# Cross attention on one core: the key projection by seven products instead of eight, in two rounds

## The reference

```python
Q = (input_Q @ W_Q).reshape(b, -1, N_HEADS, D_K).transpose(0, 2, 1, 3)
K = (input_K @ W_K).reshape(b, -1, N_HEADS, D_K).transpose(0, 2, 1, 3)
V = (input_V @ W_V).reshape(b, -1, N_HEADS, D_V).transpose(0, 2, 1, 3)
scores = jnp.einsum('bhqd,bhkd->bhqk', Q, K) / np.sqrt(D_K)
attn = jax.nn.softmax(scores, axis=-1)
context = jnp.einsum('bhqk,bhkd->bhqd', attn, V)
context = context.transpose(0, 2, 1, 3).reshape(b, -1, N_HEADS * D_V)
out = context @ W_O + input_Q
mu, var = jnp.mean(out, axis=-1, keepdims=True), jnp.var(out, axis=-1, keepdims=True)
return (out - mu) / jnp.sqrt(var + 1e-05)
```

## Time and profile before

| | us |
|---|---|
| median of 3 runs | 1601.09 |
| profiled execution, its own time | 1601.11 |
| its span (first to last instruction) | 1599.3 |
| TensorE busy | 1590.5 (99%) |
| VectorE busy | 1314.6 (82%) |
| ScalarE busy | 835.4 (52%) |
| GpSimd busy | 64.2 (4%) |

### The profile page before, as it was taken

How to read it: one execution, slowest core, us unless ns; L and a number is a source line. 1 busy time by engine, 2 the same in 40 slices (tenths; PEclk the granted TensorE clock), 3 DMA queues, 4 the chain that set the end, 5 groups by cost and what they waited for, 6 DMA issues and landing times.

```text
span 1599.3 us, 39500 instructions
## 1 busy us (share of the span) xinstructions
PE 1590.5 (99%) x17484; PEld 1073.0 (67%) x17484; DVE 1314.6 (82%) x1229; ACT 835.4 (52%) x828; POOL 64.2 (4%) x41
## 2 busy tenths in 40 slices
PE   9999999999999999999999999999999999999998
PEld 4576677766777667766677666776677766777435
DVE  7788788887888788887798878988789887888877
ACT  4445554555545555456544565445654455544653
POOL 0001000010000001000010000000000000000100
PEclk9999999999999999999999999999999999999999
DMA  4000000000000000000000000000000000000000
GB/s 162 3 2 9 1 2 9 2 10 1 10 2 1 10 1 10 2 1 9 1 10 2 2 9 2 10 2 2 9 1 10 2 9 2 1 10 2 9 2 15
DMA packets 13006, 14.26 MB, mean 9 GB/s; under 512 B 4784, under 2 KB 8624, under 8 KB 12832
## 3 DMA queue, kind: packets, MB, share of 16 engines
q1 hardware_dynamic: 12544, 11.36, 2.3%
q10 hardware_dynamic: 288, 0.33, 0.1%
HBM read 10.60 MB, written 0.59 MB: 7 GB/s over the span
## 4 chain that ended last, share of the span: by engine, by line
PE 98%; DVE 1%; ACT 0%; issue 0%; DVEq 0%; ACTq 0%
PE o_ps L484 44%; PE s_ps L467 42%; PE w_ps L549 6%; PE w_ps L532 5%; PE s_ps L616 0%; DVE inv_sum L943 0%; DVE y L976 0%; DVE stats L963 0%; PE w_ps L564 0%; DVE y L959 0%; PE w_ps L607 0%; DVE inv_sum L809 0%; DVE sums L835 0%; DVE limits L985 0%; DVE k_all L809 0%
## 5 line engine op out<-in xcount | busy, mean ns | idle before, releaser
L728 ACT ACTIVATE probs<-s_ps 128x1024 f32<-128x1024 f32 x801 | 822.5, 1027 | 737.1 <-PE s_ps L467 737.1
L835 DVE TENSOR_TENSOR sums<-sums,probs 128x1024 f32<-128x1024 f32 x785 | 968.0, 1233 | 213.7 <-ACT probs L728 205.5
L484 PE MATMUL o_ps<-probs,v_all 64*64 64x512 f32 x6408 | 942.9, 589 | 0.0
L467 PE MATMUL s_ps<-q_sb,k_all 64*64 64x512 f32 x6408 | 942.8, 589 | 0.0
L467 PEld LDWEIGHTS s_ps<-q_sb,k_all 64*64 64x64 f32 x6408 | 447.8, 133 | 238.9 <-issue 39.0
L484 PEld LDWEIGHTS o_ps<-probs,v_all 64*64 64x64 f32 x6408 | 424.8, 133 | 204.9 <-issue 33.6
L532 PEld LDWEIGHTS w_ps<-wv_sb,ctx_all 64*64 64x64 f32 x3176 | 122.4, 132 | 30.6 <-issue 1.7
L809 DVE TENSOR_REDUCE k_all<-w_ps 128x512 f32<-128x1024 f32 (+2 forms) x104 | 122.8, 1181 | 16.0 <-PE w_ps L549 14.9
L809 DVE TENSOR_REDUCE v_all<-w_ps 128x512 f32<-128x1024 f32 (+2 forms) x103 | 121.8, 1182 | 15.8 <-PE w_ps L532 15.7
L532 PE MATMUL w_ps<-wv_sb,ctx_all 64*64 64x128 f32 x3176 | 120.0, 269 | 0.1
L549 PE MATMUL w_ps<-ctx_all,wk_sb 64*64 64x512 f32 (+2 forms) x832 | 119.3, 573 | 0.0
(11 more groups left out here) (85 smaller groups left out, 119.5 us busy)
## 6 DMA issues: line engine op xcount, KB each, us to landing
inv_sum<-inv_dram SPq DMA_DIRECT2D x30, 128.0 KB, 2.9
ctx_all<-in_ctxT SPq DMA_DIRECT2D x11, 256.0 KB, 5.1
quad_rows<-quad_sums SPq DMA_DIRECT2D x60, 4.0 KB, 1.8
x_sb<-in_x SPq DMA_DIRECT2D x1, 512.0 KB, 10.1
wo_sb<-in_wo SPq DMA_DIRECT2D x1, 512.0 KB, 11.3
left_rows<-p_left SPq DMA_DIRECT2D x30, 8.0 KB
inv_left<-inv_dram SPq DMA_DIRECT2D x30, 8.0 KB
wq_sb<-in_wq SPq DMA_DIRECT2D x1, 448.0 KB, 6.4
```

The source lines that it names most:

```text
L467: last = nc.tensor.matmul(s_ps[part(half), u % 2, head * QH:(head + 1) * QH], k_all[part(head), c * P + half * DH:c * P + (half + 1) * DH] ...
L484: last = nc.tensor.matmul(o_ps[part(head), rows, :], v_all[part(rows), c, part(head)], probs[part(rows), u % RING, head * QH:(head + 1) * QH],
L728: nc.scalar.activation(probs[:, u % RING, :], s_ps[:, u % 2, :], ACT.Exp, scale=SCALE).then_inc(probs_ready, 1)
L835: nc.vector.tensor_tensor(out=sums[0:rows, t % 2, :], in0=sums[0:rows, t % 2, :], in1=probs[0:rows, u % RING, :], op=ALU.add).then_inc(sum ...
```

## The change

For the pairs 1 to 7 the 12 full key blocks are computed with Strassen's scheme: the product of the weights (2x2 parts of 64x64: input half by head) and the context (2x2 parts: input half by a set of keys) takes 7 products of parts instead of 8, with sums of parts before and differences after. Pair 0 and the tail block stay as they are.

- A block's 14 matmuls of 128 columns come in two rounds: `seven_first` (kind "r", 8 matmuls: 2 on each quarter) and, two steps later, `seven_second` (kind "k", 6 matmuls: one half of the rows has 2 on each of its quarters, the other half 1). Which half has more changes from block to block (`one = b % 2`). The value block moves from c = 2, 6, ... to c = 3, 7, .... First rounds and value blocks stand behind the step's `product`, second rounds ahead of it (`behind`); the tail key block at c = 40 also stands ahead.
- Between the rounds ScalarE copies parts to the other half of the partitions (`cross`, three activations) and GpSimd takes two differences of 128x128 (`sum_crossed`). VectorE evicts with three instructions instead of one (`take_seven`), 256 columns each; the first of them waits for GpSimd's second difference.
- The sums of context parts (`form_keys`, four GpSimd instructions a block) are made once, in pass 0, written to DRAM (`forms_dram`) and loaded again for each pair, 384 KB a block, into two buffers (`c_forms`). The sums of weights (`form_weights`, eight GpSimd instructions a pair) are made at c = 20 of the odd pass before. The new issues stand in SyncE's queue among the old ones.
- VectorE's sums stand one step ahead instead of two (`SUMS_AHEAD = 1`). GpSimd's normalization moves to c = 13 of its order. The chunks within a block change places, and `product` reads the values in the same order (`key_chunk`).

```diff
+    NEXT_STEPS = (0, 36, 38, 40, 41, 42, 44, 45)
+    SUMS_AHEAD = 1
@@ work_at
+            if by_seven(pair, at // 4 + 2) and at % 4 in (0, 2):
+                return ("rk"[at % 4 // 2], pair, at // 4 + 2)
             if at >= 0 and at % 4 == 0 and at // 4 + 2 < BLOCKS:
                 return ("k", pair, at // 4 + 2)
-            if at >= 2 and at % 4 == 2 and at // 4 + 2 < BLOCKS:
+            if at >= 2 and at % 4 == (2 if t == 0 else 3) and at // 4 + 2 < BLOCKS:
                 return ("v", pair, at // 4 + 2)
@@ gpsimd
+            def sum_crossed(pair, b):
+                n = seven_index(pair, b)
+                pool.wait_ge(crossed_ready, 3 * (n + 1))
+                m4, m3, m1 = (1, 2, 3) if b % 2 == 0 else (2, 3, 1)
+                nc.gpsimd.tensor_tensor(out=crossed[:, m4, :], in0=crossed[:, m4, :], in1=crossed[:, 0, :],
+                                        op=ALU.subtract).then_inc(crossed_summed, 1)
+                pool.wait_ge(crossed_summed, 2 * n + 1)
+                nc.gpsimd.tensor_tensor(out=crossed[:, 0, :], in0=crossed[:, m3, :], in1=crossed[:, m1, :],
+                                        op=ALU.subtract).then_inc(crossed_summed, 1)
@@ tensor
+            def seven_first(found):
+                pe.wait_ge(work_ready, READY[found] - 1)
+                pe.wait_ge(w_forms_ready, pair)
+                pe.wait_ge(c_forms_loaded[n % 2], 16 * (n // 2 + 1))
+                for i in range(2):
+                    g = part(1 - i)
+                    nc.tensor.matmul(main[g, 0, 1, :], w_form(one, 0, 1 - i), form(one, pair, b, i, 0), start=True, stop=True)
+                    nc.tensor.matmul(extra[g, 0, :], w_form(two, 5, i), form(two, pair, b, i, 2), start=True, stop=True)
+                for i in range(2):
+                    h = part(i)
+                    at = pair * P + i * DH
+                    nc.tensor.matmul(main[h, 1, 1, :], wk_sb[part(one), at:at + DH], form(one, pair, b, i, 1),
+                                     start=True, stop=True)
+                    last = nc.tensor.matmul(m1[h, :], w_form(two, 3, i), form(two, pair, b, i, 0), start=True, stop=True)
+            def seven_second(found):
+                pe.wait_ge(crossed_ready, 3 * (n + 1))
+                for i in range(2):
+                    nc.tensor.matmul(extra[part(i), 1, :], w_form(two, 4, i), form(two, pair, b, i, 1), start=True, stop=True)
+                for i in range(2):
+                    at = b * BK + 2 * i * P
+                    nc.tensor.matmul(main[part(i), 1, 0, :], w_form(one, 1, i), form(one, pair, b, i, 2), start=True, stop=True)
+                    last = nc.tensor.matmul(main[part(1 - i), 0, 0, :], w_form(one, 2, 1 - i), ctx_all[part(one), at:at + P],
+                                            start=True, stop=True)
+            def behind(found, u):
+                return found[0] in "rv" and by_seven(found[1], 0) and u % FULL_CHUNKS > 0
@@ scalar
+            def cross(pair, b):
+                act.wait_ge(work_done, COUNT["r", pair, b])
+                if n > 0:
+                    act.wait_ge(work_ready, READY["k", pair - (b == 0), (b - 1) % FULL_BLOCKS])
+                for half in range(2):
+                    nc.scalar.activation(crossed[part(1 - half), 1:4, :], apart[part(half), :, :],
+                                         ACT.Copy).then_inc(crossed_ready, 1)
+                nc.scalar.activation(crossed[:, 0, :], seven_slots(b)[2], ACT.Copy).then_inc(crossed_ready, 1)
@@ vector
+            def take_seven(found):
+                dve.wait_ge(work_done, COUNT[found])
+                dve.wait_ge(crossed_summed, 2 * (n + 1))
+                nc.vector.tensor_tensor(out=target[:, :, 0, :], in0=both, in1=main[:, :, 0, :],
+                                        op=ALU.subtract).then_inc(seven_step, 1)
+                nc.vector.tensor_reduce(out=target[:, :, 1, :], in_=main.rearrange("p j s k -> p j k s"), axis=AX.X,
+                                        op=ALU.add)
+                dve.wait_ge(seven_step, n + 1)
+                nc.vector.tensor_tensor(out=target[:, :, 0, :], in0=target[:, :, 0, :], in1=extra,
+                                        op=ALU.subtract).then_inc(work_ready, 1)
```

More of the change, by code:

```diff
@@ L265, in spread_wide, with turned_ctx, form, w_form @@
             return v_wide[part(head), :].rearrange("p (n m) -> p n m", n=PAIRS)[:, :, head * LEFT:(head + 1) * LEFT]
+        def turned_ctx(b):
+            return attn[:, PAIRS - 1, b % 2 * QH:(b % 2 + 1) * QH]
+        def form(half, pair, b, i, n):
+            at = (3 * i + n) * P
+            return c_forms[part(half), seven_index(pair, b) % 2, at:at + P]
+        def w_form(half, n, i):
+            return w_forms[part(half), n, part(i)]
+        def seven_slots(b):
+            other = w_ps[:, 1 - b % 2, :].rearrange("p (n k) -> p n k", k=P)
+            pair_at, m1_at = (2, 1) if b % 2 == 0 else (0, 3)
+            return (w_ps[:, b % 2, :].rearrange("p (j s n) -> p j s n", j=2, s=2),
+                    other[:, pair_at:pair_at + 2, :], other[:, m1_at, :])
         def banks_of(found):
@@ new lines, in store_forms, with load_forms @@
+            def store_forms(b):
+                sp.wait_ge(c_forms_ready, b + 1)
+                sp.dma_start(forms_dram[b, :, :], c_forms[:, b % 2, :]).then_inc(c_forms_stored[b % 2], 16)
+            def load_forms(pair, b):
+                n = seven_index(pair, b)
+                if n < 2:
+                    for slot in range(2):
+                        sp.wait_ge(c_forms_stored[slot], 16 * (FULL_BLOCKS // 2))
+                else:
+                    sp.wait_ge(work_done, COUNT["k", pair - (b < 2), (b - 2) % FULL_BLOCKS])
+                sp.dma_start(c_forms[:, n % 2, :], forms_dram[b, :, :]).then_inc(c_forms_loaded[n % 2], 16)
@@ new lines, in load_turned_w @@
+            def load_turned_w(pair):
+                if pair > 1:
+                    sp.wait_ge(work_done, COUNT["k", pair - 1, FULL_BLOCKS - 1])
+                for half in range(2):
+                    sp.dma_start(w_forms[part(half), 0, :], w_k[part(1 - half), pair * P:(pair + 1) * P]
+                                 ).then_inc(turned_w_loaded, 16)
+            for b in range(2):
+                load_turned(b)
+            for b in range(FULL_BLOCKS):
+                if b == LEFT_BEHIND:
+                    load_left(0)
+                store_forms(b)
+                if b + 2 < FULL_BLOCKS:
+                    load_turned(b + 2)
@@ L365, in _ @@
             sp.wait_ge(left_zeroed, 2)
             for t in range(PASSES - 1):
+                pair, h = (t + 1) // 2, (t + 1) % 2
+                if h == 0:
+                    for b in range(2, 5):
+                        load_forms(pair, b)
                 sp.wait_ge(quad_sums_ready, t + 1)
@@ L384, in _ @@
                     load_left(t + 1)
+                if h == 1 and pair + 1 < PAIRS:
+                    load_turned_w(pair + 1)
+                    for b in range(2):
+                        load_forms(pair + 1, b)
+                if h == 0:
+                    for b in range(6, FULL_BLOCKS):
+                        load_forms(pair, b)
             def general():
@@ L429, in _, with add_halves @@
             nc.gpsimd.memset(inv_left[:, :], 1.0).then_inc(left_zeroed, 1)
-            for t in range(PASSES - 1):
-                pair, h = t // 2, t % 2
+            def add_halves(t):
                 pool.wait_ge(o_a_ready, t + 1)
@@ new lines, in _ @@
+            pool.wait_ge(identity_ready, 2)
+            pool.wait_ge(left_zeroed, 2)
+            for b in range(FULL_BLOCKS):
+                form_keys(b)
+            pool.wait_ge(c_forms_ready, FULL_BLOCKS)
+            for t in range(1, PASSES):
+                for c in range(FULL_CHUNKS):
+                    if c == 0:
+                        add_halves(t - 1)
+                    found = work_at(t, c)
+                    if found is not None and found[0] == "r":
+                        sum_crossed(found[1], found[2])
+                    if c == NORM_STEP:
+                        norm(t - 1)
+                    if c == W_FORMS_STEP and t % 2 == 1 and t // 2 + 1 < PAIRS:
+                        form_weights(t // 2 + 1)
@@ L628, in _ @@
                     left_work(found)
-                elif found is not None:
-                    work(found)
+                elif found is not None and not behind(found, u):
+                    project(found)
                 product(u)
+                if found is not None and behind(found, u):
+                    project(found)
             work(("d", PASSES - 1, 0))
@@ L908, in _ @@
                 take(found)
-            for u in range(AHEAD):
+            for u in range(SUMS_AHEAD):
                 add_sums(u)
```

166 lines of the change are left out of this document (136 added, 30 removed).

## The result

| | before | after |
|---|---|---|
| median, same chip | 1601.05 us (12 runs) | 1604.46 us (12 runs) |
| ratio, 95% interval | | 1.0021 [1.0013, 1.0029] |
| profiled execution, its span | 1601.11, 1599.3 | 1603.05, 1601.3 |

A forecast was written before the change was run, and what follows sets the result against it. The prediction took TensorE, busy 99% of the span, as the bound. Its terms -3.3 + 5.6 + 4.8 + 1.8 + 1.3 = +10.2 us took 1601.1 to about 1611 us, range 1598 to 1625.

The forecast's parts named there:

- columns removed: TensorE's 84 key blocks: the half of the rows done first runs ahead (the lead), saving 0.04 a block, -3.3 us.
- tail key block: At c = 40 TensorE waits 0.80 us for the value block's eviction in each of 7 even passes, +5.6 us.
- VectorE in even passes: VectorE's extra work delays evictions in steps 2 to 11, two waits making 0.69 us a pass, +4.8 us (0 to 12).
- c = 42 of odd passes: The left-over row's sum delays a value block's eviction, so the next first round stands 0.25 us, +1.8 us (0 to 4).
- `form_keys` in pass 0: 48 GpSimd instructions among VectorE's sums, which they exclude, cost +1.3 us (0 to 12).
- what limits the lead: TensorE's wait for the value block's eviction: possible after 2.54 us, due after 2.60, so 0.05 of 0.11 comes through.
- The third rival: A faster hand-over from eviction to matmul carries the lead whole (-7.8), VectorE's waits mostly vanish: 1596 us, chance 0.12.
- four steps at 8.49 or less: Sign in the middle of an even pass that the lead is whole; the forecast itself had 8.55 us.
- The second wait: In steps 4 to 11 of even passes, from fold and inversion: assumed as large as the first, 0.34 us.
- Rival 1: TensorE's strict order or costlier short matmuls: nothing saved, 1.4 in place of -3.3, 1616 us, chance 0.15.
- Rival 2: VectorE and GpSimd lock each other, 0.25 us lost per block, 21 us more: 1632 us, chance 0.14.
- Rival 4: Tail stall as computed, lead whole, no other stalls: 1600 us; or a 3.3 gain without later stalls: 1604; chance 0.14.

The follow-up runs named there:

- e1: The changed kernel with the tail key block of pairs 1 to 7 moved from c = 40 to c = 41: 1598.33 us, ratio 0.9983 to the kernel before.
- e8: The changed kernel with GpSimd's two differences between the rounds narrowed from 128 to 8 columns (keys wrong): 1601.97 us, ratio 1.0007 to the kernel before.
- e11: e1 with only the left-over row moved, to c = 30 of even and c = 44 of odd passes: 1597.55 us, ratio 0.9978 to the kernel before.
- e9: The kernel before with VectorE's sums one step ahead instead of two, nothing else changed: 1600.44 us, ratio 0.9998.
- e12: e11 with the transpose also moved from c = 2 to c = 3: 1601.23 us, ratio 1.0003 to the kernel before.
- e2: The changed kernel with the same half of the rows heavier in every block, no exchange (keys wrong): 1609.72 us, ratio 1.0057 to the kernel before.
- e3: The changed kernel with the second round's two matmuls of the lighter half issued twice: 1613.29 us, ratio 1.0081 to the kernel before.
- e4: The changed kernel with the four GpSimd sums per block in pass 0 replaced by writes of zeros (keys wrong): 1603.64 us, ratio 1.0018 to the kernel before.
- e5: The changed kernel with VectorE's sums two steps ahead again: 1614.39 us, ratio 1.0088 to the kernel before.
- e7: e1 with transpose, fold, inversion, GpSimd's normalization and left-over row moved to later steps: 1621.3 us, ratio 1.013 to the kernel before.

## Why the prediction was wrong

Per pair, in us: the lead gives 12 x 0.09 = 1.08. Of the waits, e1 shows 0.84 for the tail, e8 and the steps 0.32 for c = 4, e11 against e1 0.16 for c = 42. 195.43 - 195.03 + 1.08 = 1.48 are there in all, so 0.16 is left for c = 7, 11 and 16 (the longer steps there show 0.42; the steps behind them are up to 0.16 shorter than their like, which fits a half that catches up where only the other one stood, but no run tested it). Times 7, beside the forecast:

| term | forecast | measured |
|---|---|---|
| columns removed | -3.3 | -7.6 |
| tail key block | +5.6 | +5.9 |
| VectorE in even passes | +4.8 | +3.4 |
| c = 42 of odd passes | +1.8 | +1.1 |
| `form_keys` in pass 0 | +1.3 | +0.5 (up to 1.5 in other profiles) |
| sums one step ahead, first step (e9) | not priced | -0.35 |
| sum | +10.2 | +3.0 (up to 4.0) |

- **The step that failed is what limits the lead.** The direction was right, and the mechanism (an eviction that returns just in time) too; its size was not. The prediction had 1.29 us from the value block to its eviction and 0.19 from eviction to matmul. Measured are 1.25 (476.95 to 478.20) and at most 0.12. With 0.15 of lead the first was to hold the leading half 0.10 too long; the 0.04 and the 0.07 that were too much are just that much, and the lead of 0.16 goes through. So the columns bring -7.6 and not -3.3. I had added a weight load of 0.13 between the eviction and the matmul. The trace of the changed kernel shows that the matmul starts within 0.06 of its load, and when TensorE stands, with it (L740, above): a load's duration isn't time ahead of its matmul. The earlier trace rows could not show it, since that matmul was due later anyway. The third rival had named this very condition, and its price for the columns (-7.8) was right; it got 0.12 because I took a bound for a value. Its total (1596) was not: the tail's wait and VectorE's stayed. The sign I had set for it, four steps at 8.49 or less, was too sharp: they take 8.505 with the lead whole.
- **The tail** was right: 0.80 forecast, 0.80 in the trace, 0.84 by e1. (Its bounds, with hand-overs of 0.05 and 0.25, come to 4.6 and 6.0 and not to 4.5 and 6.3.)
- **VectorE** was right at c = 4 (0.34 against 0.32), in its size and in its chain: the eviction by seven waits for GpSimd's second difference (I had it start 0.54 after the second round, it starts 0.40 after, 414.99 against 414.33 + 0.27 = 414.60 for the end of its last matmul), the transpose stands behind it, and the wait goes without either of them (e8, e12). The second wait, which I had assumed at the same size without working it out, was too high: 0.16 for c = 7, 11 and 16 together.
- **Rival 1** (strict order) is refuted by e2 and e3: the exchange of the roles and the matmuls left out change the time by 5.3 and 8.8 us. The rule of the Trainium skill that the prediction weighed ("TensorE: Matmul & The Clock Gate", Part 3: Packing small matmuls) does not hold for this trace: L674 starts at 474.38 ahead of L776 at 474.43.
- **Rival 2** (lock) is there in the records, 1.18 us for a difference of 0.46 alone, and hidden in most blocks: VectorE waits 63 times for L613, 0.42 us at most, and the middle steps don't change in e8. In even passes it has its share in the wait at c = 4 (e8), besides what it costs in pass 0 (e4).
- **No stretch of the eviction by seven.** It never meets the differences, since it waits for them, but 7 of its 84 first instructions run wholly beside a normalization of GpSimd, as this one:

```profile
441.10 0.42 DVE L1091 TENSOR_TENSOR k_all<-crossed,w_ps 128x256 f32<-128x256 f32 x1 [0.42 <-POOL crossed L613]
```

```profile
440.95 1.28 POOL L562 TENSOR_TENSOR attn<-o_b,inv_sum 128x512 f32<-128x512 f32 x1
```

  They last 0.42 us as the others do, and the normalization 1.28 where the earlier trace rows has 1.27. By the rule cited from the Trainium skill ("SBUF — State Buffer", Who interferes with whom) they should not stretch beside GpSimd, and this trace agrees.
- **Rival 4** (half of it) names 1604 us, and the measured 1604.5 lies on it by luck: that variant has the lead cut to 3.3 us and no stalls but the tail's. Its other variant, with the lead whole and the tail as computed (1600 us), has two of the three main terms right and lacks VectorE's 4.5 us.
- **The sums one step ahead** I had not priced. They bring 0.35 us alone (e9, within the noise), and save some 10 us here (e5): without this part the change would have lost 0.9%.
- Right too: no wait for `crossed` at TensorE, none for `c_forms` (until e7 moved the inversion), ScalarE's copies hidden.

Open: whether the transpose or the fold could leave the crowded steps altogether, what the two short rounds lose 0.08 us on (e3), and what decides in an execution whether `form_keys` costs 0.4 us or more.

## What to carry to other kernels

When a gain is a few hundredths of a microsecond that must pass under a wait, the sum turns on the hand-over: take it from a place where the waiting engine really stood, and give the case its own chance when the margin is smaller than what the row leaves open. After a change, look for the one place where the period breaks (here the tail block, seven times 0.8 us): it was worth more than the whole loss. And before a piece is moved on an engine that is full, write down what waits behind it on that engine and on every queue that its result passes.

## What the runs showed of the hardware

- The halves of the rows of TensorE run on by themselves: 0.16 us apart over whole passes of the kernel before at no cost (groups of eight last 1.19 us and follow each other after 0.86), and here with work of 4 and 2 instructions per quarter that is balanced only over two blocks.
- A weight load begins 0.06 us after the eviction that it waits for. Where TensorE stood for it (L740), the matmul begins with its load, at 496.49.
- GpSimd's instruction of two SBUF inputs begins on the record and then stands for VectorE's sum: the second difference with 8 columns takes 0.20 us alone and 1.25 beside a sum, and ends 0.06 after it (e8).
